# A recommender tower on one core: thirteen batched field pairs, other places for the transposes, and half-adds on VectorE

## The reference

```python
e = jnp.stack([tbl_0[ids[:, 0]], ..., tbl_39[ids[:, 39]]], axis=1)   # 512 x 40 x 64
viW = jnp.einsum('bpd,pde->bpe', vi, W)      # vi = e[:, i_idx], 780 pairs
z = jnp.einsum('bpe,bpe->bp', viW, vj)
h = jnp.concatenate([z, dense_ctx], axis=1)
h = jnp.maximum(h @ W_top1 + b_top1, 0.0)    # 796 -> 512
h = jnp.maximum(h @ W_top2 + b_top2, 0.0)    # 512 -> 256
y = h @ W_top3                               # 256 -> 1
```

## Time and profile before

| | |
|---|---|
| timed runs, median (lowest, highest) | 350.28 us (350.03, 350.73) |
| the profiled execution | 350.38 us |
| its span, first to last instruction | 348.40 us |
| mean granted clock of PE | 0.976 |
| PE busy | 320.4 us (92%) |
| VectorE busy | 250.3 us (72%) |
| GpSimd busy | 228.4 us (66%) |
| ScalarE busy | 174.0 us (50%) |

### The profile page before, as it was taken

The page is one execution under the profiler, slowest core; times in us unless marked ns, Lnnn a source line. Parts: engine busy times, 40 slices in busy tenths (PEclk is TensorE's granted clock), DMA queues, the critical chain, the costliest instruction groups (busy, mean ns, idle before and its releaser), DMA issues.

```text
span 348.4 us, 5290 instructions
## 1 busy us (share of the span) xinstructions
PE 320.4 (92%) x1528; PEld 112.4 (32%) x1528; DVE 250.3 (72%) x252; ACT 174.0 (50%) x1312; POOL 228.4 (66%) x192
## 2 busy tenths in 40 slices
PE   0699898529999999999999999999999999999997
PEld 0133432113333333333333333333333333344432
DVE  2385696506887989799899899999998999900000
ACT  1001210000198572876947958795934999190032
POOL 6777777777777734898778884799773994700000
PEclk9999999958999999999999999999999999999969
DMA  6843453323333324933323242322221000000000
GB/s 166 250 149 94 118 131 90 79 49 87 103 95 96 88 77 131 304 83 80 101 67 87 72 109 62 84 68 64 69 66 49 0 3 0 3 0 0 0 0 0
DMA packets 17862, 27.63 MB, mean 79 GB/s; under 512 B 4901, under 2 KB 5029, under 8 KB 17834
## 3 DMA queue, kind: packets, MB, share of 16 engines
q1 hardware_dynamic: 9770, 17.86, 17.8%
q0 software_dynamic: 4608, 4.73, 6.8%
q10 hardware_dynamic: 3456, 4.72, 4.5%
HBM read 22.57 MB, written 0.00 MB: 65 GB/s over the span
## 4 chain that ended last, share of the span: by engine, by line
PE 73%; POOL 16%; issue 6%; DVE 3%; DMA 1%; ACT 0%; DVEq 0%
PE ps_t L539 36%; PE ps_z L561 15%; POOL rows L320 11%; PE ps_t L522 10%; PE ps_t L586 6%; POOL wide_rows L320 5%; PE ps_t L621 3%; DVE prod L447 3%; PE ps_e L501 2%; PE ps_e L586 2%; DMA rows<-in_tbl,ids_sb 1%; DMA ids_sb<-in_ids_t 1%; PE ps_t L627 1%; DVE batched L461 0%; ACT z L393 0%
## 5 line engine op out<-in xcount | busy, mean ns | idle before, releaser
L447 DVE TENSOR_TENSOR prod<-ps_t,E 128x1024 f32<-128x1024 f32 x160 | 184.7, 1217 | 35.6 <-PE ps_t L539 32.0
L372 ACT ACTIVATE batched<-batched 128x64 f32<-128x64 f32 x640 | 152.9, 241 | 23.6 <-DVE prod L447 21.1
L539 PE MATMUL ps_t<-E,w_sb 64*128 64x512 f32 x640 | 156.1, 617 | 1.0 <-DVE prod L447 0.2
L320 POOL DMA_INDIRECT rows<-in_tbl,ids_sb x128 | 121.7, 951 | 38.1 <-issue 37.6
L372 ACT ACTIVATION_READ_ACCUMULATOR batched<-batched 128x1 f32 x640 | 120.0, 188 | 0.0
L327 POOL TENSOR_TENSOR prod<-prod 128x1024 f32<-128x1024 f32 x38 | 89.0, 2371 | 30.0 <-DVE prod L447 29.9
L539 PEld LDWEIGHTS ps_t<-E,w_sb 64*128 64x128 f32 x640 | 55.9, 187 | 90.7 <-issue 60.9
L349 ACT ACTIVATE E<-ps_e 128x512 f32<-128x512 f32 x18 | 10.7, 597 | 102.4 <-PE ps_e L501 79.6
L561 PE MATMUL ps_z<-prod,quads 128*32 128x512 f32 x408 | 58.4, 600 | 0.0
L461 DVE TENSOR_TENSOR batched<-ps_t,wide_rows 128x1024 f32<-128x1024 f32 x40 | 46.2, 1218 | 5.7 <-PE ps_t L522 5.7
L522 PE MATMUL ps_t<-w_sb,E 64*128 64x512 f32 x160 | 37.3, 604 | 0.2 <-DVE batched L461 0.2
(11 more groups left out here) (41 smaller groups left out, 61.2 us busy)
## 6 DMA issues: line engine op xcount, KB each, us to landing
w_sb<-in_w_units SPq DMA_DIRECT2D x50, 256.0 KB, 2.8
E<-E ACTq DMA_DIRECT2D x72, 64.0 KB, 2.6
rows<-in_tbl,ids_sb POOLq DMA_INDIRECT x128
w_sb<-in_w SPq DMA_DIRECT2D x7, 256.0 KB
prod<-in_ids_by_field SPq DMA_DIRECT2D x2, 512.0 KB, 9.1
prod<-in_tbl SPq DMA_DIRECT2D x3, 312.5 KB
w_sb<-in_w SPq DMA_DIRECT2D x1, 512.0 KB
wide_rows<-in_tbl,ids_sb POOLq DMA_INDIRECT x16, 4.8
```

The lines of the kernel that those rows point to most:

```text
L320: pool.indirect_dma_start(rows_of(u, b)[:, f * DIM:(f + 1) * DIM], None, tables[2 * k + f], bass.IndirectOffsetOnAxis(ap=ids_sb[:, col:col ...
L372: last = act.activation(products, products, ACT.Copy, accum_out=zt[:, b, at:at + 1])
L447: dve.tensor_tensor(prod[:, n % P_RING, s, :, :], ps_t[:, step % STEPS, :, :], multiplier, ALU.mult).then_inc(product_ready, 1)
L539: last = pe.matmul(ps_t[:, step % STEPS, j, :], w_sb[at:at + DIM, m % W_RING, col:col + P], E[at:at + DIM, slot_of(pairs_of(n)[s][j]), :], ...
```

## The change

Four things change. Three more pairs (14, 9 and 0) are batched, and the batched units begin behind the fourth unit and stand at positions given by a list; there are 74 groups in place of 80, so six groups (three units) become three batched units. Pairs are turned one group ahead of their first group up to F11 and two ahead from F12 on (one and four before, with the switch at F8). VectorE adds the halves of six couples, each group's two groups later, and GpSimd those of 19 couples, beginning at couple 14 in place of 12. ScalarE takes a sum at every group as long as there is one. The weights' ring has six buffers in place of eight, and gathers are placed up to 14 groups ahead in place of 12. The last chunk of `z` has five couples only.

```diff
-W_RING = 8
+W_RING = 6
-GATHER_LEAD = 12
+DVE_BEHIND = 2
+GATHER_LEAD = 14
-BATCHED = (12, 10, 8, 7, 6, 5, 4, 3, 2, 1)
-BATCHED_FROM, BATCHED_EVERY = 7, (13, 3)
+BATCHED = (14, 12, 10, 9, 8, 7, 6, 5, 4, 3, 2, 1, 0)
+BATCHED_AT = (4, 6, 10, 13, 17, 20, 24, 27, 31, 34, 38, 41, 45)
...
-ADDED_COUPLES = (12, 13, 15, 18, 20, 21, 23, 25, 26, 27, 28, 30, 32, 33, 34, 35, 36, 37, 38)
+POOL_COUPLES = (14, 15, 16, 18, 19, 20, 21, 23, 24, 25, 26, 27, 28, 30, 31, 32, 33, 34, 35)
+DVE_COUPLES = (6, 7, 8, 10, 11, 13)
...
 def ahead(u):
-    return 1 if u < 8 else 4
+    return 1 if u < 12 else 2
...
-                if n in ADDED:
+                if n in ADDED_BY_POOL:
                     add_halves(n)
...
-                elif kind == "group" and left and at % 7 in (0, 2, 3, 5):
+                elif kind == "group" and left:
                     sum_batched(*left.pop(0))
...
+            def add_halves(n):
+                dve.wait_ge(product_ready, FIRST_STEP["group", n] + 2)
+                dve.tensor_tensor(prod[:, n % P_RING, 0, :, :], prod[:, n % P_RING, 0, :, :],
+                                  prod[:, n % P_RING, 1, :, :], ALU.add).then_inc(halves_added_by_dve, 1)
...
                     multiply(at)
+                    if at - DVE_BEHIND in ADDED_BY_DVE:
+                        add_halves(at - DVE_BEHIND)
...
-                    if g in ADDED:
-                        pe.wait_ge(halves_added, ADDED.index(g) + 1)
+                    if g in ADDED_BY_POOL:
+                        pe.wait_ge(halves_added, ADDED_BY_POOL.index(g) + 1)
+                    elif g in ADDED_BY_DVE:
+                        pe.wait_ge(halves_added_by_dve, ADDED_BY_DVE.index(g) + 1)
```

More of the change, by code:

```diff
@@ L70 @@
 NU = NC + NB
-CHUNKS = NG // PER_CHUNK
+CHUNKS = -(-NG // PER_CHUNK)
 B_PAIRS = 2 * WIDE * NB
@@ L75 @@
 DENSE_AT = B_REST
-ADDED_COUPLES = (12, 13, 15, 18, 20, 21, 23, 25, 26, 27, 28, 30, 32, 33, 34, 35, 36, 37, 38)
-ADDED = [n for n in range(NG) if n // 2 in ADDED_COUPLES]
+POOL_COUPLES = (14, 15, 16, 18, 19, 20, 21, 23, 24, 25, 26, 27, 28, 30, 31, 32, 33, 34, 35)
+DVE_COUPLES = (6, 7, 8, 10, 11, 13)
+ADDED_BY_POOL = [n for n in range(NG) if n // 2 in POOL_COUPLES]
+ADDED_BY_DVE = [n for n in range(NG) if n // 2 in DVE_COUPLES]
+ADDED = sorted(ADDED_BY_POOL + ADDED_BY_DVE)
 def arrival(k):
@@ L123, in order @@
         units += n % 2
-        if n % 2 and j < NB and arrival(BATCHED[j]) < u and units >= (
-                BATCHED_FROM + BATCHED_EVERY[0] * j // BATCHED_EVERY[1]):
+        if n % 2 and j < NB and arrival(BATCHED[j]) < u and units >= BATCHED_AT[j]:
             yield "batched", j
@@ L235, in tower_kernel @@
         halves_added = sem("halves_added")
+        halves_added_by_dve = sem("halves_added_by_dve")
         two_reduced = sem("two_reduced")
@@ L466, in copy_z @@
             def copy_z(c):
-                dve.wait_ge(two_reduced, PER_CHUNK // 2 * (c + 1))
+                dve.wait_ge(two_reduced, min(PER_CHUNK // 2 * (c + 1), NC))
                 dve.tensor_copy(z[:, c, :], ps_z[:]).then_inc(z_copied, 1)
@@ L562, in reduce_two @@
                                              start=(q == 0 and s == 0),
-                                             stop=(q == PER_CHUNK // 2 - 1 and (s == 1 or g in ADDED)))
+                                             stop=((q == PER_CHUNK // 2 - 1 or n == NG - 2)
+                                                   and (s == 1 or g in ADDED)))
                 last.then_inc(two_reduced, 1)
```

## The result

The changed kernel takes 353.89 us (median of 4 runs, 353.34 to 355.2), the kernel before 350.5 on the same chip: 1.0102 times as long, 95% interval 1.0068 to 1.0135. It is slower, as forecast, and inside the range, but by 3.4 us where 8.6 were forecast. The profiled execution took 353.51 with a span of 351.4, 3.0 more than before. Those 3.0 are two differences of opposite sign: the last product ends at 302.37 + 9.19 = 311.56, 6.55 later than before, and the tail behind it takes 39.8 instead of 43.4.

A forecast was written before the change was run, and what follows sets the result against it. PE bounds the kernel before, ScalarE's queue the changed one: start 67.5 plus 218.5 and F19's copy gives 286.6, last product 313.6, plus the 43.4 tail 357.0 of span, 359.0 us in all (8.6 slower); range 353 to 367.

The forecast's parts named there:

- ScalarE's queue, 218.5 us from B0's first product to F19's copy: ScalarE: 48 sums of 3.83, 11 copies with DMAs and one without, 218.5 us without a gap, so F19's copy begins at 286.0.
- The start: B0's first product, from which ScalarE's queue is counted: at 67.5, after F6's turn at 56.98 and groups 6 and 7.
- the smaller waits that were named: Waits for copies at F9 (some 5 us), F14 and F16, said to cost nothing beyond ScalarE's queue.
- B12 and the eight groups after F19, 27.0: From F19's copy at 286.6 to the last product at 313.6: 1.7 + 6.2 + 18.2 + 0.9, B12's steps at 1.2 GHz.
- VectorE's adds, 1.13 each: VectorE's 12 new adds of two SBUF operands, taken at its multiply's 1.13 from start to start: 13.6 us.
- The rival by which they stretch to 2.37: VectorE's adds cost GpSimd's 2.37, 12 us more ahead of B4, ScalarE idles for it: 366 to 371; chance 12%.
- Reductions, 14.9 less: PE's reductions: 488 records fall to 392 at 0.155 each, 14.9 us less for PE.
- the 43.4 in the sum: The tail from the last product to the end of the span, taken as unchanged at 43.4 us.
- the forecast's own range of 354.7 to 363: Range of the main case (76%): full clock at both places gives 354.7, ScalarE's waits at F10, F12 and B4 the upper end.
- the signs to look for: If right: F19's copy near 287, PE and VectorE idle ahead of B2 and B12, ScalarE's chain share up, reductions near 61 us.
- the first rival: ScalarE keeps up and VectorE's pace decides: B12 at 269.8, last product 294.4, time about 340; chance 9%.
- allowed 0.1 to 0.3 us for each of 12 gathers: GpSimd's gathers beside VectorE's adds, by the shared SBUF interfaces: at most 4 us on F12 to F15, sum unchanged.

The follow-up runs named there:

- the first: Changed kernel with the four E4 DMAs of each pair issued from SP's queue instead of ScalarE's: 344.26 us, ratio 0.983 to the kernel before.
- second: Changed kernel with 8 instead of 16 ACTIVATEs in each sum: 343.77 us, ratio 0.9814 to the kernel before.
- fourth experiments: Changed kernel with pairs from F12 on turned four groups ahead instead of two: 348.78 us, ratio 0.9966 to the kernel before.

## Why the prediction was right in kind and wrong in size

- *ScalarE's queue, 218.5 us from B0's first product to F19's copy.* Right: 66.75 to 285.05 is 218.3, and the first, second and fourth experiments shift the end by shortening the queue or by taking F19's place forward in it. The start was 0.75 early: F6 could be turned at 56.48 instead of 56.98, and groups 6 and 7 took 4.84 behind that wait (clock 0.62 from 56.9 to 61), where 3.31 + 1.82 were charged. Of the smaller waits that were named, the one at F9 came (4.20); at F14 and F16 PE waited less than 0.1.
- *B12 and the eight groups after F19, 27.0.* They took 311.56 - 285.62 = 25.9. PE ran at the lower clock for two of B12's steps only (L534, 8 records in 3.46), not for all four.
- *VectorE's adds, 1.13 each.* Right: 1217 ns of busy time each, as the multiply has, and 1.13 from start to start (93.60 to 94.73). The rival by which they stretch to 2.37 fell.
- *Reductions, 14.9 less.* 10.9 less, since 0.155 was a mean over all 488 records: the 80 of `halves` took 0.215 each and all stayed (17.2 us in both kernels), and the 96 of `quads` that went took 0.114 each. They were not what set the end.
- *"Behind the last product PE, the adds ... and the top layer are the same; the transposes of the sums have more rows and the same columns."* This is the step that failed, the 43.4 in the sum. The tail was not the same: 39.8 in its place. The prediction saw the additional rows and valued them at nothing, since the columns stay the same. It didn't look at the granted clock of before's tail, 0.78 and 0.75, which was there to be read. The kernel before with 96 rows has a tail of 39.8 too, so in the profiled executions this is the whole of the 3.6.

The balance: the profiled execution is 359.0 - 353.5 = 5.5 below the forecast, of which the tail is 3.6, B12 and what follows 1.1, and the start with the queue 1.0; what lies around the span was 0.1 more. With the tail right the forecast would have been 355.4. The three large errors all go the same way. The measured 353.89 lies below the forecast's own range of 354.7 to 363, and that the wider range still holds it is in part luck: no case that was reckoned leads to it.

Two of the signs to look for were wrong as well. ScalarE's share of the chain was to rise from 0%, and it didn't, though its queue set the end; and the reductions were to be near 61 us and took 64.7. F19's copy was the sign that told the cases apart, as 285.05 against the 272 or less of the first rival.

A rival was mis-sized too: with ScalarE free, 340 was expected and 343.8 to 344.3 measured. It took VectorE's pace for the whole bound. From 99 to 150 us that holds, but elsewhere PE's reductions keep VectorE waiting, 0.82 at a time behind a full couple's and 0.60 behind an added couple's with a turn, as at 277.23 above. In the kernel with half sums VectorE was busy 50.84 of 51 us up to 150, but 146.0 of 153 from there to 303, where PE was busy 150.4:

```profile
150.00:303.00 153.00, 150.44 (x754) 50.19 (x750) 146.00 (x129) 70.31 (x551) 123.12 (x73) 1.00 0.22 60
```

From B0 to B12 VectorE waited for PE twelve times there, 8.8 us in all, and its last product came at 301.9 where the rival had 294.4. The two engines bound in turns. That the rival's time is only 4 us off is luck too, for its sum holds the tail of 43.4.

The Trainium skill, "TensorE: Matmul & The Clock Gate", section "Why this matters for your kernels", says that a matmul over 32 rows takes as long as one over 128. By it 48 and 96 rows would cost the same here; at a clock of 1.00 nothing here contradicts it, but the stretch with 48 rows did not keep that clock, and the measurement decides: 3.6 us.

## What to carry to other kernels

An engine that is busy half the time and has 0% of the chain can still be the next bound: add up its queue, DMA issues included, between the first input and the last output that others wait for, and compare that with the time in which the others would do it. Before leaving a tail out of the sum as unchanged, read its granted clock: a step that runs below full clock can get faster by a change of shape alone. Work moved to spare an engine pays only if the receiving engine has room in the same stretch.

## What the runs showed of the hardware

With the same wait of 0.7 us ahead, the number of rows of a few matmuls decided the granted clock behind them: sixteen records of the following layer took 9.40 us behind eight records on 48 rows (clock 0.75) and 6.87 behind the same eight on 96 (clock 1.00). Why is open.

GpSimd's gathers grew longer beside VectorE's adds. Groups by line on GpSimd, 93 to 146 us, of the kernel after (count, busy us, mean ns):

```profile
L325 POOL DMA_INDIRECT rows<-in_tbl,ids_sb x37 | 43.0, 1161 | 11.3 <-issue 11.3
```

The same of the kernel without the adds:

```profile
L325 POOL DMA_INDIRECT rows<-in_tbl,ids_sb x42 | 39.7, 944 | 12.8 <-issue 12.8
```

1161 ns with the adds, 944 without; the adds themselves did not stretch. The mean hides that single gathers grew. GpSimd's timeline in the kernel after, around VectorE's add at 116.69 (1.22 us):

```profile
115.63 0.94 POOL L325 DMA_INDIRECT rows<-in_tbl,ids_sb  x1 [0.30 <-issue]
116.88 1.85 POOL L325 DMA_INDIRECT rows<-in_tbl,ids_sb  x1 [0.30 <-issue]
119.03 0.94 POOL L325 DMA_INDIRECT rows<-in_tbl,ids_sb  x1 [0.30 <-issue]
```

Ten adds lie in that stretch, and ten gathers, one beside each, took 1.37 to 1.85 us; the other 27 took 0.94 or 0.95. Behind it, GpSimd's first two adds, beside VectorE's last two, took 6.66 us together, where one takes 2.37 on average before.

The prediction had weighed this by the Trainium skill, "GPSIMD Engine Reference", Specifications (shared SBUF interfaces, contention with VectorE instructions of two SBUF inputs), and allowed 0.1 to 0.3 us for each of 12 gathers. Here the trace agrees with the page, and the gathers cost more, 0.4 to 0.9 us each: 37 x 0.217 = 8.0 us in all. It fell on GpSimd, which had it to spare: it stands in the chain of the kernel after only up to 54 us.
